# Out-projection of an attention block as three passes over rounded halves, with the keys of the second batch loaded into the first batch's place

## What is computed

```python
q = jnp.einsum('bim,ghmd->bghid', x, w_aq)        # B 2, T 1024, M 256, G 4, H 4, D 128
k = jnp.einsum('bim,gmd->bgid', x, w_ak)
v = jnp.einsum('bim,gmd->bgid', x, w_av)
q = _rope(q); k = _rope(k)
s = ...                                            # causal scores
p = jax.nn.softmax(s, axis=-1)
o = jnp.einsum('bghij,bgjd->bghid', p, v)
r = jnp.einsum('bghid,ghdm->bim', o, w_ao)         # the out-projection
x = _layernorm(x + r)
x = _layernorm(x + experts(x) + shared(x))
```

## Time and profile before

| | |
|---|---|
| median of 3 runs | 1080.67 us (1075.64 to 1081.76) |
| the profiled execution, its own time | 1073.27 us |
| its span | 1071.5 us |
| TensorE (PE) busy | 965.9 us, 90% |
| weight loads (PEld) busy, beside PE | 739.3 us, 69% |
| VectorE (DVE) busy | 681.1 us, 64% |
| ScalarE (ACT) busy | 488.6 us, 46% |
| GpSimd (POOL) busy | 371.8 us, 35% |
| mean granted clock of TensorE | 0.957 |

### The profile page before, as it was taken

How to read it: one execution, slowest core, us unless ns; L and a number is a source line. 1 busy time by engine, 2 the same in 40 slices (tenths; PEclk the granted TensorE clock), 3 DMA queues, 4 the chain that set the end, 5 groups by cost and what they waited for, 6 DMA issues and landing times.

```text
span 1071.5 us, 16751 instructions
## 1 busy us (share of the span) xinstructions
PE 965.9 (90%) x5240; PEld 739.3 (69%) x5240; DVE 681.1 (64%) x1703; ACT 488.6 (46%) x1083; POOL 371.8 (35%) x334
## 2 busy tenths in 40 slices
PE   8999979989999999999979999999999998559745
PEld 6888867667787778776767667888787776336412
DVE  5989853775766675757565668575857666424326
ACT  4012124555656564645544456564645544125402
POOL 4878863234323121021244332312031112126811
PEclk9999988999999999999979999999999999769968
DMA  8696765463222111111243224351112133978687
GB/s 254 228 289 218 250 230 159 127 165 110 73 64 61 60 52 58 45 33 50 85 133 90 84 74 132 87 156 45 56 31 69 44 79 99 274 214 194 86 279 284
DMA packets 137303, 137.24 MB, mean 128 GB/s; under 512 B 18065, under 2 KB 108805, under 8 KB 137216
## 3 DMA queue, kind: packets, MB, share of 16 engines
q1 hardware_dynamic: 84064, 98.33, 30.1%
q10 hardware_dynamic: 43872, 29.50, 9.4%
q0 software_dynamic: 9280, 8.34, 4.5%
HBM read 86.44 MB, written 63.05 MB: 140 GB/s over the span
## 4 chain that ended last, share of the span: by engine, by line
PE 67%; DVE 10%; issue 8%; SPq 5%; DMA 5%; ACT 2%; POOL 2%; ACTq 1%; DVEq 0%; POOLq 0%
PE s_ps L1116 14%; PE ring L1126 9%; PE o_ps L1146 8%; PE o_ps L1143 8%; PE ring L1155 7%; PE s_ps L1095 6%; PE ring L1095 5%; DVE neg_max L1319 2%; SPq L759 2%; PE s_ps L1209 2%; PE o_ps L1095 2%; SPq L655 1%; PE s_ps L1119 1%; DVE pt_lo L1253 1%; DMA inverses<-inv_t 1%
## 5 line engine op out<-in xcount | busy, mean ns | idle before, releaser
L1319 DVE TENSOR_REDUCE neg_max<-s_ps 128x1 f32<-128x128 f32 (+7 forms) x256 | 191.6, 750 | 137.6 <-PE s_ps L1119 131.8
L961 ACT ACTIVATE probs<-s_ps,neg_max 128x128 f32<-128x128 f32 (+7 forms) x256 | 189.7, 741 | 142.3 <-DVE neg_max L1319 127.8
L1116 PE MATMUL s_ps<-kt,qt_hi 128*128 128x512 f32 (+3 forms) x768 | 235.2, 388 | 6.0 <-ACT probs L961 3.9
L824 POOL TENSOR_TENSOR qt_lo<-q_raw,qt_hi 128x512 fp32r<-128x512 f32 x64 | 82.1, 1283 | 319.3 <-ACT qt_hi L875 319.0
L1126 PE MATMUL ring<-ident,probs 128*128 128x128 f32 x1152 | 177.5, 277 | 9.2 <-DVE pt_lo L1253 5.1
L875 ACT ACTIVATE pt_hi<-ring 128x512 fp32r<-128x512 f32 x168 | 99.8, 596 | 181.8 <-PE ring L1126 173.6
L1116 PEld LDWEIGHTS s_ps<-kt,qt_hi 128*128 128x128 f32 x768 | 139.7, 194 | 54.9 <-issue 30.2
L1253 DVE TENSOR_TENSOR pt_lo<-ring,pt_hi 128x512 fp32r<-128x512 f32 x168 | 115.4, 687 | 62.2 <-ACT pt_hi L875 56.7
L1126 PEld LDWEIGHTS ring<-ident,probs 128*128 128x128 f32 x1152 | 129.1, 142 | 33.7 <-issue 14.5
L1146 PE MATMUL o_ps<-pt_hi,v 128*128 128x512 f32 x336 | 145.9, 435 | 1.4 <-DVE pt_lo L1253 0.9
L1116 PE MATMUL s_ps<-kt,qt_lo 128*128 128x512 f32 (+3 forms) x384 | 134.6, 350 | 0.0
(11 more groups left out here) (201 smaller groups left out, 1378.8 us busy)
## 6 DMA issues: line engine op xcount, KB each, us to landing
qk_rows<-prods SPq DMA_DIRECT2D x80, 256.0 KB, 2.8
q_raw<-qk_rows ACTq DMA_DIRECT2D x128, 128.0 KB
inv_row<-inverses SPq DMA_DIRECT2D x64, 256.0 KB
fsum<-sums SPq DMA_DIRECT2D x48, 256.0 KB, 8.1
sums<-blank SPq DMA_DIRECT2D x16, 640.0 KB
wexp<-in_L_ffn_w_gate_dram SPq DMA_DIRECT2D x32, 192.0 KB, 5.0
wexp<-in_L_ffn_w_up_dram SPq DMA_DIRECT2D x32, 192.0 KB, 5.2
wexp<-in_L_ffn_w_down_dram SPq DMA_DIRECT2D x32, 192.0 KB, 6.3
```

Of the source, the lines that this page charges most:

```text
L961: act.activation(probs[:, u % 2, h, 0:blocks(u) * P], s_ps[:, n % 2, score_cols(n)], ACT.Exp, bias=neg_max[:, n % 8:n % 8 + 1], accum_out= ...
L1116: pe.matmul(s_ps[:, n % 2, c + a:c + e], q[qp], k[kp][:, a:e], start=(qp == kp == 0), stop=(qp == 1 and not last))
L1319: dve.tensor_reduce(neg_max[:, n % 8:n % 8 + 1], s_ps[:, n % 2, score_cols(n)], AX_X, ALU.max, negate=True).then_inc(max_ready, 1)
```

## The change

The out-projection now works on rounded halves. `omul` writes `ot_raw` (2 units). A new step `osplit` makes `ot_hi` on ACT and `ot_lo` on POOL. `w_ao` is loaded group by group by SP into `wo_raw` (which shares its place with the raw rotation tables), three groups during the projections and the last at the start of attention; ACT rounds each (`wo_hi`), DVE or, for the last, POOL subtracts (`wo_lo`). Before, POOL's queue loaded all four groups during units 1 to 4. `outproj` makes 48 matmuls: `ot_hi` x `wo_hi`, `ot_hi` x `wo_lo`, `ot_lo` x `wo_hi`.

To make room there is one `kt`. The keys of batch 1 are loaded group by group when the last unit of that group in batch 0 (28 to 31) has its scores, and are split at units 30, 31, 32 and 33. Expert weights are no longer loaded into `kt[0]` during batch 1: where the homes were filled up to pair 7 (before unit 60), 8, 10, 12, 13 (units 60 to 63), 17 (after `omul` of unit 62) and 28 (at `outproj` of tile 15), they are now filled up to 0, 2, 4, 5, 7, 10 and 23, and the last 5 pairs are issued behind the last `z_sb` store.

```diff
-KSPLIT_AT = [14, 16, 18, 20]
-K_LOAD_AT = [(8, 2), (9, 2), (10, 2), (11, 2)]
+LAST_FIRST = NT * G - G
+KSPLIT_AT = [(LAST_FIRST + 2 + g, 0) for g in range(G - 1)] + [(LAST_FIRST + G + 1, 2)]
+WO_LOAD_AT = [("rope", 1, 1, 1), ("rope", 2, 0, 1), ("rope", 2, 3, 1), ("score", 1, 0)]
+WO_SPLIT_AT = [("proj", 1, 3, 0, 1), ("proj", 2, 2, 0, 1), ("proj", 3, "K", 1, 1), ("exp", 2, 2)]
...
     def product():
         u, j = waiting.pop(0)
         seq.append(("pv", u, j))
+        if j == 0 and u >= 1:
+            osplit(u - 1)
...
+            if step == ("outproj",):
+                osplit(tile * G + G - 1)
@@ SP @@
+                if s in WO_LOAD_AT:
+                    g = WO_LOAD_AT.index(s)
+                    sp.wait_ge(tab_ready, 2 * HT)
+                    used(sp, wo_ready, g)
+                    sp.dma_start(wo_raw[:, :, :], w_ao[g].rearrange("h d m -> d h m")).then_inc(wo_loaded, 16)
+                if s[0] == "ptrans" and LAST_FIRST <= s[1] < LAST_FIRST + G and s[2] == 0:
+                    g = s[1] - LAST_FIRST
+                    sp.wait_ge(scores_ready, H * (s[1] + 1))
+                    used(sp, k_ready, G + g if g else 0)
+                    load_k(sp, 1, g)
...
-                        load_homes(kt[0], v_sb[0], *[kt[1][:, 0, :, :]] * (g + 1))
+                        load_homes(v_sb[0], *[kt[:, 0, :, :]] * (g + 1))
...
-                    load_homes(kt[0], v_sb[0], kt[1], v, q_raw, qt_hi, qt_lo, probs, pt_hi, pt_lo)
+                    load_homes(v_sb[0], kt, v, q_raw, qt_hi, qt_lo, probs, pt_hi, pt_lo)
@@ POOL @@
+                if s[0] == "osplit":
+                    u = s[1]
+                    pool.wait_ge(ot_hi_ready, u + 1)
+                    pool.tensor_tensor(ot_lo[:, u % G, :], ot_raw[:, u % 2, :], ot_hi[:, u % G, :].bitcast(F32),
+                                       ALU.subtract).then_inc(ot_ready, 1)
@@ ACT @@
+                if kind == "osplit":
+                    u = s[1]
+                    act.wait_ge(o_ready, u + 1)
+                    if u >= G:
+                        act.wait_ge(attn_ready, u // G)
+                    split(ot_hi[:, u % G, :], ot_raw[:, u % 2, :]).then_inc(ot_hi_ready, 1)
@@ PE, outproj @@
-                    for h in range(G * H):
-                        if h % H == 0:
-                            pe.wait_ge(o_ready, G * i + h // H + 1)
-                        ins = pe.matmul(bank(s)[:, 0:M], ot[:, h // H, (h % H) * P:(h % H + 1) * P], wo[:, h, :],
-                                        start=(h == 0), stop=(h == G * H - 1))
+                    for op, wp, g, h in itertools.chain(itertools.product((0,), range(2), range(G), range(H)),
+                                                        itertools.product((1,), (0,), range(G), range(H))):
+                        if wp == h == 0:
+                            pe.wait_ge((ot_hi_ready, ot_ready)[op], G * i + g + 1)
+                        ins = pe.matmul(bank(s)[:, 0:M], (ot_hi, ot_lo)[op][:, g, h * P:(h + 1) * P],
+                                        (wo_hi, wo_lo)[wp][:, wo_at(g), h, :], start=(op == wp == g == h == 0),
+                                        stop=(op == 1 and g == G - 1 and h == H - 1))
@@ DVE, omul @@
-                    if i >= 1:
-                        dve.wait_ge(attn_ready, i)
+                    used(dve, ot_ready, u - 1)
```

99 lines of the change are left out of this document (58 added, 41 removed).

## The result

Six runs of the changed kernel have a median of 1090.13 us (1087.66 to 1095.77), and those of the kernel before, taken with them, 1079.14 (1075.36 to 1082.13). The ratio on record is 1.0136, with a 95% interval of 1.0103 to 1.0169: the change makes the kernel slower, by about 15 us. (The two medians themselves lie 11.0 us apart, so the size is less certain than the direction.) I had forecast 1074.1 us and given slower a chance of 0.13. The profiled execution took 1090.55 us, 1088.7 of it the span: 17.3 us more than the span of before.

A forecast was written before the change was run, and what follows sets the result against it. TensorE, busy 90% of the span, was taken as the bound, with latencies and full DMA queues elsewhere. Out-projection gains of 9.6 and 5.4 and 3 at attention's start, less costs, gave -6.6 us: 1080.67 to 1074.1, range 1064 to 1084.

The forecast's parts named there:

- the matmuls: Each out-projection: 48 matmuls 118 ns apart, 5.7 us where 6.91 were taken, so 1.2 us shorter if nothing holds it.
- Taking the four key splits of batch 1 out of units 14 to 20 gains nothing: Batch 0's attention: removing these splits gains nothing, since ACT and POOL work is hidden in large tiles.
- `ot_hi`: Tiles 0, 1, 2, 8, 9 and 10: TensorE stalls 0.3 us for the last group's half, leaving 0.9 us gain each.
- tile 7's own out-projection: TensorE waits 1.6 us for ACT's ot_hi and 1.2 for POOL's ot_lo: 1.6 us slower instead of 1.2 faster.
- the start of attention: Three w_ao loads leave it, inverses land sooner: 3 us gained (0 to 5.1); the fourth split costs 1 us.
- Three splits in the projections cost ACT 1.05 and DVE 1.59 us each; eight PSUM banks cover them: 0.5 us (0 to 2).: Projections: the three w_ao splits are covered by PSUM banks and cost 0.5 us (0 to 2).
- hidden for groups 0 to 2: Keys' reload for batch 1: load and splits of 3 + 1 + 2.4 us hide in units of 15 us and more.
- the end: After the last pv: z_sb lands 4.3 us later, and slot rows sharing with five pairs cost 3 us (0 to 10.8).
- Two pairs ... 4.3 us later for the landing of z_sb: The end: 13 pairs instead of 11 ahead of the last stores, 1.18 MB more at 272 GB/s, 4.3 us.
- The first comes 1 us later and the second stalls it for 2 more: 3 us: The end: slot-row loads share evenly with five pairs; first load 1 us later, second stalls TensorE 2 more.
- the fourth, slower: Batch switch: stalls at tile 7 hold the clock low 10 us more, losing 5 to 8 us; 1087 us, chance 0.13.

The follow-up runs named there:

- e4: The changed kernel with the last group's twelve matmuls at the end of each out-projection's 48; ratio 1.0095 to the kernel before.
- e2: The changed kernel with the first and third split of w_ao in the projections some steps later; ratio 1.0084 to the kernel before.
- e6: The changed kernel with key splits of groups 0 to 2 three heads later, group 3's behind tile 7's out-projection and rstd; ratio 1.0130 to the kernel before.
- e5: The kernel before with its expert pairs issued at the places and in the numbers of the changed kernel; ratio 1.0144 to the kernel before.
- e1: The changed kernel with the last five expert pairs issued only when the slot rows of the first 14 pairs have landed; ratio 1.0105 to the kernel before.
- e7: The changed kernel with e1's edit and eight more expert pairs moved behind the slot rows; ratio 1.0126 to the kernel before.
- e10: The changed kernel with the last z_sb stored from ACT's queue instead of SyncE's; ratio 1.0109 to the kernel before.
- e12: e11 with e10's edit added; ratio 0.9986 to the kernel before.
- e11: The changed kernel with e2, e4 and e6, and an edit to load two expert pairs early, which loaded none; ratio 1.0041 to the kernel before.
- e3: The changed kernel with group 0's key split three heads later and group 3's behind tile 7's out-projection; ratio 1.0163 to the kernel before.
- e14: e12 again, timed beside e13; ratio 0.9972 to the kernel before.
- e13: The kernel before with e10's edit alone; ratio 0.9974 to the kernel before.

## Why the prediction was wrong

**Right: the matmuls.** The pace is 120 ns where 118 was taken, 5.75 us in the chain for 5.7. From tile 11 to 14 the tiles gave 0.7 to 1.2 us each for a forecast of 1.2. The Trainium skill's "TensorE: Matmul & The Clock Gate", section "Back-to-back issue gap", has 109 ns for an isolated matmul of 256 columns and says itself that a stream of weight loads and matmuls goes by both; the 109 ns that the prediction sets beside its sum are too low for this stream.

**Wrong, in my favour: "Taking the four key splits of batch 1 out of units 14 to 20 gains nothing".** From tile 2 to 3 and from 3 to 4, where those splits stood, the kernel gained 2.06 and 1.97 us; from tile 10 to 11 and 11 to 12, the same steps without splits, 0.96 and 0.99. Some 2 us came from here, so that -5.7 us against a forecast of -6.3 from tile 0 to 6 is in part luck: they made up for the small tiles, below. The kernel before shows why, VectorE and then GpSimd:

```profile
331.57 2.29 DVE L1420 TENSOR_SCALAR row<-chose_s,top_inv 128x64 f32<-128x64 f32 x1
```
```profile
331.44 2.37 POOL L819 TENSOR_TENSOR kt<-kt 128x1024 fp32r<-128x1024 f32 x1 [4.48 <-ACT kt L875]
```

The same operation took 0.26 us in the changed kernel, with GpSimd idle beside it. VectorE is held to the end of GpSimd's key subtraction, and TensorE then waits 0.7 us for the `probs` that follow. It is the effect that cost 1.72 us at the batch switch, and it could have been read ahead of the change.

**Right in mechanism, small in size: `ot_hi`.** The stall of 0.3 us was 0.5 to 0.8 at tiles 0, 1, 2, 9 and 10, and 2.0 at tile 8 in two pieces. Tiles 0, 1 and 9, for which 0.9 us each were forecast, gained nothing. e4 shows that an order of the matmuls removes these stalls.

**Right: tile 7's own out-projection**, 8.31 us between starts, forecast about 8.5, with both waits.

**Right: the start of attention.** Of the 9.8 us by which the projections ended late 7.0 were left at tile 0's out-projection: 2.8 us regained, where the forecast was 3 less 1 for the fourth split. VectorE's waits for `inv_row` went from 5.1 us to 1.3, as forecast.

**Wrong: "Three splits in the projections cost ACT 1.05 and DVE 1.59 us each; eight PSUM banks cover them: 0.5 us (0 to 2)."** It was 9.8. I priced the splits, not the load that ACT has to wait for, nor what is queued behind it: a load that I took for 5 us landed after 12.2, behind a stretch where the DMA engines are full to 0.89 (50 to 80 us). The banks could not cover that, because the `xt_hi` and `xt_lo` of the next matmuls stood behind the split and its subtraction. The stall gave 4.2 us of the 9.8, the half clock that followed it 2.9, the end of the projections the rest. e2 removes the stall at this place and ends the projections 3.9 us earlier, a figure with a spread of some 2 us in it; what is left of the cost after e2 is not explained.

**Wrong: "hidden for groups 0 to 2."** The work of the key splits is hidden, not its side effects. GpSimd's subtraction held VectorE at the one moment at which TensorE waits for VectorE. Without it and the splits at tile 7 (e6) the stretch from tile 6 to 9 is 6.6 us shorter. Start by start against e6, the changed kernel loses 1.9 us at the normalisation and 2.1 at tile 7's two stalls; the rest is spread over the stages between and behind them and isn't assigned.

**Mis-sized: the end.** "Two pairs ... 4.3 us later for the landing of z_sb" came out as 4.3. "The first comes 1 us later and the second stalls it for 2 more: 3 us" was 4.6 and 2.15, 6.7 in all: the second part was right, the first was not. The engines did share, packet for packet, in line with the Trainium skill's "DMA: Bandwidth & Descriptors", section "Queues, rings and completion order", as I had read it. But I set 1 us for the first load, where its first packet came 2.5 us later after the issue than before and the rest at a shared rate: 7.6 us instead of 3.0. The two of 972 KB went from 6.4 to 14.1.

**What the price of the end was.** I followed the chain through the end and priced each link for two more pairs ahead of the last store. e5 shows the whole of it: seven pairs more pass at the end, 4.1 MB, 15 us at the 272 GB/s of the earlier trace rows, and e5's tail is 14.7 us longer. In e1, e7 and e10 another order of the same transfers wins 1 to 3 us by the ratios, and in e12 against e11 5 to 6. So the bytes are in line with the size of the loss, but a bound by their sum alone is not shown. Nor is it shown how much of a gain ahead of the end arrives: the tails of the seven kernels that end alike spread from 168.8 to 172.5 us, in no order by the start of tile 15 (e3 starts it at 920.8 and takes 171.7, the changed kernel at 919.5 and takes 169.2). What the pairs cost can be seen from e14 against e13: 8.9 us of gain at tile 15, 0.5 at the end, with seven pairs late in the one and early in the other.

The chances: the case that came true is the fourth, slower, but not by its mechanism, since the clock of tile 7 to 8 stayed at 0.82. The stretch from tile 14 to 15, 0.2 us longer than before where 1.2 shorter was forecast, is the clock too: from 904.3 to 907.7 us it is halved, and TensorE falls 1.6 us behind the kernel before, which has the full clock there. What set this off stays open, and so does the 0.7 us behind the slot rows.

## What to carry to other kernels

When a change takes memory, ask which early transfers lived in it. Where the end of a kernel is a stretch of full DMA engines, price what has to pass through it in bytes beside the links of its chain: seven late pairs cost here as much as the whole change.

A split is three things: its time, the arrival of what it reads, and all that is queued behind it on its engine. A stall of 4.2 us cost 7.1 here, because the clock was halved for 6.8 us behind it.

Check in the trace that an edit did what it says: one that was to load two pairs early loaded none, which the start of the first pair's DMA tells at once. And where a chain names a transfer, look which one of its kind it is.

## What the runs showed of the hardware

VectorE's `row<-y_sb` takes 0.40 to 0.61 us alone, 1.14 to 1.36 beside one GpSimd subtraction that began just ahead of it, and 3.45 beside two that followed each other without a gap, and it ends 0.15 us after the last of them. The Trainium skill, "SBUF — State Buffer", section "Who interferes with whom", has the two engines share a pair of ports that one holds for a whole instruction; the trace agrees, and adds that VectorE did not get in between GpSimd's two instructions.

Two DMA queues that are full at once, one with weights and one with slot rows, moved 2.23 and 1.76 MB in the same 13 us, and a load of 324 KB took 7.6 us instead of 3.0. From 967 to 970 us each moved 492 packets.

Behind the stall of 5.01 us in the projections TensorE was granted half the clock (0.50 from 85.1 to 91.9 us, 1.2 instead of 2.4 GHz), and the same matmuls fell 2.9 us behind those of the kernel before, which had the full clock there.
